# Window attention with paired value products, a third probability buffer and two transposes moved

## The reference

```
xn = layernorm(x over channels) * g1 + b1
windows of 8 x 8 pixels after a roll by -4, -4
q, k, v = xn @ qkv_w.T + qkv_b            3 heads of 8 channels
attn = softmax(q * 8**-0.5 @ k.T + relative bias + mask of shifted windows)
x1 = x + roll_back(attn @ v @ proj_w.T + proj_b)
y = layernorm(x1 over channels) * g2 + b2
...
```

## Time and profile before

| what | us |
|---|---|
| median of 3 runs | 244.88 |
| lowest and highest of them | 244.81, 248.58 |
| the profiled execution's own time | 243.31 |
| its span, from the first to the last instruction | 241.2 |
| PE busy | 222.5 |
| DVE busy | 161.9 |
| ACT busy | 137.0 |
| POOL busy | 128.0 |

### The profile page before, as it was taken

The page is one execution under the profiler, slowest core; times in us unless marked ns, Lnnn a source line. Parts: engine busy times, 40 slices in busy tenths (PEclk is TensorE's granted clock), DMA queues, the critical chain, the costliest instruction groups (busy, mean ns, idle before and its releaser), DMA issues.

```text
span 241.2 us, 7789 instructions
## 1 busy us (share of the span) xinstructions
PE 222.5 (92%) x3242; PEld 110.2 (46%) x3242; DVE 161.9 (67%) x282; ACT 137.0 (57%) x225; POOL 128.0 (53%) x166
## 2 busy tenths in 40 slices
PE   7759789999999989997999999999999989999971
PEld 4336557575758566675544444443323222222210
DVE  4587999898998979699469343434558794544321
ACT  3547575677868685843363323232465655888760
POOL 8145746566969887679999942244000020354451
PEclk9999999999999999999999999999999999999998
DMA  6940000030121474646464666773000002334121
GB/s 178 312 117 3 3 4 4 20 86 3 44 64 39 135 236 116 243 120 227 114 215 134 243 177 246 239 274 115 0 0 0 4 20 70 81 88 103 33 57 41
DMA packets 12520, 25.37 MB, mean 105 GB/s; under 512 B 6649, under 2 KB 8001, under 8 KB 10758
## 3 DMA queue, kind: packets, MB, share of 16 engines
q1 hardware_dynamic: 11462, 23.31, 30.9%
q0 software_dynamic: 1024, 1.58, 2.9%
HBM read 18.78 MB, written 3.15 MB: 91 GB/s over the span
## 4 chain that ended last, share of the span: by engine, by line
PE 78%; DVE 8%; issue 5%; POOL 2%; ACT 2%; DMA 1%; SPq 1%; POOLq 0%; DVEq 0%; ACTq 0%
PE psum L623 12%; PE psum L624 11%; PE psum L568 9%; PE psum L579 5%; PE psum L597 5%; PE psum L769 5%; PE psum L760 3%; PE psum L750 3%; PE psum L691 3%; PE psum L699 3%; PE psum L528 3%; PE psum L741 3%; DVE biased L1012 3%; PE psum L524 3%; PE psum L614 2%
## 5 line engine op out<-in xcount | busy, mean ns | idle before, releaser
L470 POOL TENSOR_TENSOR diff<-biased,mx 128x768 f32<-128x768 f32 x32 | 47.1, 1471 | 24.9 <-DVE mx L1016 23.9
L1139 DVE TENSOR_TENSOR gated<-psum,gel 64x512 f32<-64x512 f32 x32 | 22.0, 693 | 30.4 <-ACT gel L916 30.3
L1012 DVE TENSOR_TENSOR biased<-psum,pk 128x768 f32<-128x768 f32 x32 | 30.5, 952 | 8.3 <-PE psum L568 8.2
L916 ACT ACTIVATE gel<-psum 64x512 f32<-64x512 f32 x32 | 18.8, 590 | 29.6 <-PE psum L624 29.6
L841 ACT ACTIVATE pt<-psum 128x768 f32<-128x768 f32 x32 | 25.9, 808 | 15.3 <-PE psum L579 15.1
L623 PE MATMUL psum<-sta,pk 108*128 108x512 f32 x64 | 33.1, 598 | 0.1
L624 PE MATMUL psum<-stb,pk 108*128 108x512 f32 x64 | 32.7, 592 | 0.0
L1016 DVE TENSOR_REDUCE mx<-biased 128x12 f32<-128x768 f32 x32 | 30.5, 953 | 1.1
L568 PE MATMUL psum<-kmv,stq 32*64 32x192 f32 x512 | 28.1, 334 | 3.1 <-DVE biased L1012 2.0
L298 POOL DMA_DIRECT2D out<-yo x30 | 15.0, 505 | 24.8 <-DVE yo L1227 24.8
L579 PE MATMUL psum<-pk,diff 64*128 64x64 f32 x384 | 19.0, 231 | 4.3 <-POOL diff L470 3.6
(11 more groups left out here) (102 smaller groups left out, 363.8 us busy)
## 6 DMA issues: line engine op xcount, KB each, us to landing
sta<-scratch SPq DMA_DIRECT2D x24, 288.0 KB
stb<-scratch SPq DMA_DIRECT2D x24, 288.0 KB
xtok<-xt SPq DMA_DIRECT2D x8, 192.0 KB, 4.0
xin<-xw SPq DMA_DIRECT2D x8, 192.0 KB, 5.8
out<-yo POOLq DMA_DIRECT2D x30, 48.0 KB, 1.9
x<-x1s SPq DMA_DIRECT2D x28, 48.0 KB
pk<-pack SPq DMA_DIRECT2D x1, 971.5 KB, 6.6
scratch<-ytok SPq DMA_DIRECT2D x4, 192.0 KB, 4.0
```

The costliest lines, as they stand in the source:

```text
L470: g.tensor_tensor(diff[:, t % 2].rearrange("q g w n -> q (g w) n"), scores_of, mx[:, t % 2].unsqueeze(2).to_broadcast([128, 4 * NH, WT]), ...
L916: a(gel[:, u % 4, :], bank(u % 4)[0:64], ACT.Gelu).then_inc(gelu_ready, 1)
L1012: v.tensor_tensor(biased[:, slot].rearrange("q (p s) -> q p s", p=2), banks, wt("rpb").unsqueeze(1).to_broadcast([128, 2, 2 * NH * WT]), A ...
L1139: v.tensor_tensor(gated[64 * (b % 2):64 * (b % 2) + 64, b // 2, c * CH:(c + 1) * CH], bank(u % 4)[64:128], gel[:, u % 4, :], ALU.mult).the ...
```

## The change

The probability buffer `pt` gets three slots in place of two, and `exps(t)` waits for the value product of quarter t - 3 in place of t - 2. On PE the value products of quarters 0 and 1 stand together at the end of quarter 1, those of 2 and 3 at the end of quarter 3. `turn_x1(m - 2)` moves from quarter 1 to the start of quarter 0, behind `make_k(m + 1)`. `project(m - 1)` and behind it `turn_xhat(m + 2)` move to the start of quarter 2, ahead of `turn` and `scores`. `make_v(m + 1)` moves from quarter 0 to quarter 1, behind `turn_out(m - 1)`. Bank 6 now goes from `make_q` to `turn_x1` to `make_v` to `turn_xhat` to `make_q`, and the waits follow that. On ACT `take_v(m + 1)` moves behind `exps(4m + 2)`. On DVE `centre(1, m - 2)` moves ahead of `ahead(1)`, and `variance(0, m + 2)` behind it.

```diff
-        pt = sb(att, "pt", [128, 2, 2, 2 * NH * WT])
+        pt = sb(att, "pt", [128, 3, 2, 2 * NH * WT])
@@ mix(m, l)
-                        x = mm(o[...], pt[:, t % 2, ...],
+                        x = mm(o[...], pt[:, t % 3, ...],
@@ tensor: attend(m)
                     if l == 0 and not last:
                         make_k(m + 1)
+                    if l == 0 and m >= 2:
+                        if last:
+                            pe.wait_ge(cen2_ready, m - 2)
+                        else:
+                            pe.wait_ge(stq_ready, m + 2)
+                        turn_x1(m - 2)
+                    if l == 2 and m >= 1:
+                        project(m - 1)
+                    if l == 2 and m + 2 < NCH:
+                        pe.wait_ge(val_ready, m + 2)
+                        turn_xhat(m + 2)
                     if l == 2 and last:
                         pe.wait_ge(folded, 1)
                         pe.wait_ge(biased_ready, 4 * NCH)
@@
                         turn(t + 1)
                     if t + 3 < 4 * NCH:
                         scores(t + 3)
-                    if l == 0 and not last:
-                        make_v(m + 1)
-                    if l == 1 and m >= 2 and not last:
-                        pe.wait_ge(val_ready, m + 2)
-                        turn_x1(m - 2)
-                    if l == 0 and last:
-                        pe.wait_ge(cen2_ready, m - 2)
-                        turn_x1(m - 2)
                     if l == 1 and m >= 1:
                         turn_out(m - 1)
-                    if l == 2 and m >= 1:
-                        project(m - 1)
                     if l == 3 and last:
                         pe.wait_ge(cen2_ready, m - 1)
                         turn_x1(m - 1)
-                    if l == 2 and m + 2 < NCH:
-                        if m >= 2:
-                            pe.wait_ge(cen2_ready, m - 1)
-                        else:
-                            pe.wait_ge(val_ready, m + 2)
-                        turn_xhat(m + 2)
+                    if l == 1 and not last:
+                        wait(pe, cen2_ready, m - 1)
+                        make_v(m + 1)
                     if l == 3 and m + 2 < NCH:
                         make_q(m + 2)
-                    mix(m, l)
+                    if l % 2:
+                        mix(m, l - 1)
+                        mix(m, l)
@@ scalar: exps(t)
-                wait(act, mixed, t - 1)
+                wait(act, mixed, t - 2)
-                a(pt[:, t % 2], turned_banks, ACT.Exp).then_inc(probs_ready, 1)
+                a(pt[:, t % 3], turned_banks, ACT.Exp).then_inc(probs_ready, 1)
@@ scalar: attend(m)
                     take_k(m + 1, (1, 2))
+                exps(4 * m + 2)
+                if not last:
                     take_v(m + 1)
-                exps(4 * m + 2)
                 if m + 2 < NCH:
                     root(0, m + 2)
@@ vector: attend(m)
                     divide(m - 1, 1)
-                if last:
+                if m >= 2:
                     centre(1, m - 2)
+                ahead(1)
                 if m + 2 < NCH:
                     variance(0, m + 2)
-                ahead(1)
...
                 if last:
                     variance(1, m - 2)
-                elif m >= 2:
-                    centre(1, m - 2)
                 if m + 3 < NCH:
                     add_up(0, m + 3)
```

More of the change, by code:

```diff
@@ L596, in mix @@
                     for c in range(4):
-                        x = mm(o[32 * c:32 * c + 32, at:at + VW], pt[:, t % 2, c // 2, WT * k + 32 * (c % 2):WT * k + 32 * (c % 2) + 32],
+                        x = mm(o[32 * c:32 * c + 32, at:at + VW], pt[:, t % 3, c // 2, WT * k + 32 * (c % 2):WT * k + 32 * (c % 2) + 32],
                                val[:, m % 2, l, p, c // 2, h, :], start=True, stop=True)
```

## The result

The changed kernel takes **271.5 us** in the median of four runs (270.44 to 275.55), the kernel before 245.29 in the runs beside it. The ratio is **1.106**, 95% interval 1.100 to 1.112. Ratios are taken from the runs within 1.5% of the fastest of their kernel, so without the 275.55. The forecast was 268, range 261 to 273, slower.

A forecast was written before the change was run, and what follows sets the result against it. PE was taken to bound the attention, DVE close behind. Chunk terms summed to +24.1 us on the profiled 243.31, giving 267.4; the median of runs was 1.57 above that execution; 268 was said, range 261 to 273.

The forecast's parts named there:

- chunk 0: First chunk, no projection, but input transposes wait for variance and root: between 0 and +3.1 us, taken as +2.0.
- chunk 1: Second chunk, without centring: 15.9 us against a mean of 13.05, taken as +3.1, bounds 2 to 4.
- chunks 2 to 5: Middle chunks: 17.04 us each, 68.2 against 52.2 in all, +16.0.
- chunk 6: Chunk without root, queries or input: take_out follows take_v, next scores at about 14.2 against 11.2 us, +3.0.
- chunk 7: Last chunk, with few of these steps: 0, bounds -0.5 to +0.5 us.
- The chain over variance, root and take_out: Middle chunk: later DVE variance delays root and take_out on ACT; projection starts at 8.26 us, PE idle 1.95.
- Scores cannot follow scores in under 1.96: Shared score banks: 0.95 to bias add plus 1.01 to next scores; quarter 3's scores lose 0.63 us.
- Bank 6: Middle chunk's first half: make_v waits until centring frees the bank, starting at 4.68 us, not 3.3.
- PE's own work: Reordered products on PE: pairs save 0.26 us a chunk, keys before x1 transposes 0.11; about 0.3 less without waits.
- The third buffer earns nothing but is needed: Third probability buffer: earlier exponentials gain nothing, as nothing waited for them, but without it the pairs would hold them up.
- rival 3: Clock falls as well: half of PE's 12.5 us a chunk at 1.2 GHz, 295 us or more; chance 0.04.
- Convolutions, "nothing there waited long": After the chunks: convolutions begin later by the sum and are PE's own; extra time for first images' loads earns nothing.

The follow-up runs named there:

- The runs with one edit each: Changed kernel with either DVE's variance put back ahead of centre and ahead, or ACT's take_v put behind root and take_out: ratio 1.098 each.
- the run with the added products: Changed kernel with two probability buffers, plus two unread 512-column products on PE ahead of each projection: ratio 1.145.
- the one with both edits: Changed kernel with variance early on DVE and take_v behind root and take_out on ACT: ratio 1.079, median 266.6 us.

## Why the prediction was right

The mechanism came as forecast: undisturbed chunks take 16.90 to 16.99 for 17.04, with the projection held by the same chain. That the total came out within 4 us owes something to the falls of the clock and the late rows of the convolutions being small, as neither was in the sum. And the sum itself has a slip: 267.4 + 1.57 is 269.0, where 268 was said.

Against the profile, from the start of the same scores in both kernels:

| stretch | forecast | measured |
|---|---|---|
| chunk 0 | +2.0 | +2.0 |
| chunk 1 | +3.1 | +3.3 |
| chunks 2 to 5 | +16.0 | +16.9, of it 1.3 clock |
| chunk 6 | +3.0 | +3.3 |
| chunk 7 | 0 | +1.1 |
| convolutions and the rest | 0 | +1.9 |

- *The chain over variance, root and take_out*: right in place and size (8.12 for 8.26), and shown: adding its first link to the kernel before costs 0.7 us in a middle chunk, and taking both late things away gives 1.1 us. Putting work back ahead of the projection gives some 4%, the score banks' part included. That take_v is a second chain of nearly equal length was not in the prediction; it had taken the root's alone, though its own numbers, 4.68 + 0.93 + 0.99 + 0.6 + 0.6, gave about 7.8. The runs with one edit each showed both.
- *Scores cannot follow scores in under 1.96*: measured 1.96 (80.14 to 82.10). In quarter 0 it was 2.18, by the keys' copies, as allowed for. With other work between, the bracket is gone and 2.79 lie there; that run covered the chain too, so the 0.6 us of the score banks wasn't separated.
- *Bank 6*: the values wait for centring, 4.60 for 4.68, with brackets to show it. In the changed kernel its cost is hidden, but by 0.36 us only, the room ahead of the root. With variance early the wait was 0.46 longer and bank 6 itself held the projection, at 8.26.
- *PE's own work*: 0.13 for a changeover holds for the pair behind the queries (a pitch of 0.96) and failed for the pair behind the values: a pitch of 1.10 in the run with the pairs alone, and in the changed kernel a duration of 1.26 where the other has 1.03 (1.05 in chunks 0 and 1). Why is open. Keys before transposes took 0.96 for 0.94.
- *The third buffer earns nothing but is needed*: right. What going without it costs was not in the prediction: 6% more, and filling the stops alone gave back two fifths of that.
- *The clock*, rival 3 with 0.04: it did come in part. In chunk 2 the level fell behind stops of 0.78 and 0.85 with 0.4 us of products between, and the chunk took 1.3 us more. It happened again near 140 us, where chunk 7's +1.1 lies. The price of the rival was far too high, since it took half of all work at 1.2 GHz and here two stretches of 3.4 us were (61.05 to 64.46 and 139.56 to 142.97).
- *Convolutions, "nothing there waited long"*: that was the step that failed. Some 1.5 of the last row's 1.9 us are one stop. In the kernel before, POOL finished image 2's second half at 154.5 and its first product began at 154.94, so 0.4 us was all the room. After:

```profile
182.78 1.10 PE L623 MATMUL psum<-sta,pk 108*128 108x512 f32 x2 [1.37 <-issue]
```

```profile
181.38 1.31 POOL L458 TENSOR_SCALAR stb<-stb,pk 108x64 f32<-108x64 f32 x3 [3.02 <-DMA stb<-scratch]
```

Counted from the end of chunk 7 in the table (127.44 before, 153.76 after), the rows of the image were issued 0.5 us later than before, and they landed some 1.3 us later behind their issue; why they took longer is open. POOL's last mask on them ends at 182.69 and PE's first product on them begins at 182.78, though the view names no releaser ("issue"). The sum of the prediction, made against the profiled execution, was 267.4 us; measured there is 271.17. The rows of the table exceed their forecasts by 0.2, 0.9, 0.3, 1.1 and 1.9, together 4.4; the time ahead of the first scores and outside the span is 0.6 shorter, which leaves the 3.8.

## What to carry to other kernels

Where PE is 99% busy, a group that stands between two others is also the time in which another engine works: before two groups are put side by side, ask what was being done behind the one that moves away. Follow a moved product's input back through the in-order queues of all engines, and list every chain that ends at the wait; undoing one of two nearly equal chains shows nothing. And price a repeated wait on TensorE twice: as time, and by what the groups behind it cost if the clock falls.

## What the runs showed of the hardware

**A stop can cost as much in the clock as in itself, but not each time.** With two buffers, a chunk with a stop of 2.63 us took 20.50 us where the level fell to 1.2 GHz and 18.20 where it stayed at 2.4. The length of the one stop didn't decide it. Stops of 1.53 to 1.58 kept the level in four of the changed kernel's chunks. One stop of 1.66 us stands in every profile, ahead of the first turn (17.62 in the kernel before); the level fell within 1 us behind it in four of the thirteen and stayed in nine. So a single execution carries an accident of a us or two, which the experiments above can't tell from an edit of that size. Filling the stops took most of the falls away. The Trainium skill, TensorE: Matmul & The Clock Gate, section HAM oscillation, describes a kernel that loses its clock to repeated waits of TensorE; by it, filling the waits should give time back, and the run with the added products agrees: ratio 1.175 to 1.145, medians 289.9 to 285.0 us.

**Stops marked "issue" at fixed places of PE's instruction stream.** In the thirteen profiles there are 22 such stops between 20 and 150 us. All came at a count of PE's records (weight loads and products, from the first on) that leaves 193 when divided by 256, counted in the traces: 4033 in the kernel before (0.61 us), 1985 in the changed one (0.78), 1985, 2753 and 3777 with projection put back (1.28, 1.28, 0.34). They are 0.2 to 1.8 us long. Of the some 270 such counts in that stretch most show no stop of PE. Many of the groups around the stops are the densest, values and then a pair of value products, 256 records in 1.64 us. That PE waits there for its next block of instructions is my reading and wasn't tested. In the changed kernel the count 2753 falls into the wait for the projection. The versions that shorten or remove the wait show more of these stops: 2.3 us in the one with both edits, 2.9 with projection put back, against 0.78. That is a part of why they gave back less than expected.
